# Score maxima six items ahead instead of four, with the turn one key tile earlier, in a gated cross-attention kernel

## The reference, cut to what matters

```
q = (query @ Wq).reshape(b, sq, 32, 32).transpose(0, 2, 1, 3)
k = (key @ Wk).reshape(b, sk, 8, 32).transpose(0, 2, 1, 3)
v = (value @ Wv).reshape(b, sk, 8, 32).transpose(0, 2, 1, 3)
k, v = repeat(k, 4), repeat(v, 4)
scores = einsum('bhqd,bhkd->bhqk', q, k) * 32 ** -0.5
probs = softmax(scores)
out = einsum('bhqk,bhkd->bhqd', probs, v)
```

## Time and profile before

| | |
|---|---|
| median of 3 runs | 966.67 us |
| runs | 962.91, 966.88, 966.67 us |
| profiled execution | 963.45 us, span 961.6 us |
| busy in the span | PE 875.3, DVE 667.5, POOL 527.4, ACT 421.4 us |
| mean granted TensorE clock | 0.973 |
| turns of attention (L1399) | first at 393.6, last at 788.8 us |

### The profile page before, as it was taken

The page is one execution under the profiler, slowest core; times in us unless marked ns, Lnnn a source line. Parts: engine busy times, 40 slices in busy tenths (PEclk is TensorE's granted clock), DMA queues, the critical chain, the costliest instruction groups (busy, mean ns, idle before and its releaser), DMA issues.

```text
span 961.6 us, 15794 instructions
## 1 busy us (share of the span) xinstructions
PE 875.3 (91%) x4784; PEld 353.9 (37%) x4784; DVE 667.5 (69%) x974; ACT 421.4 (44%) x730; POOL 527.4 (55%) x236
## 2 busy tenths in 40 slices
PE   3988998858889989699999999999999998999998
PEld 2656746323344434122222222222222221444443
DVE  4789867899875479677778777777778860155522
ACT  3333423433131112376776767777767777011000
POOL 4322345585330034378788888888888888321200
PEclk9999999878999999799999999999999999999999
DMA  5942222011111265234455445554444444222342
GB/s 176 354 161 88 103 88 66 1 45 44 44 55 67 85 183 164 64 86 94 103 118 118 96 97 118 118 118 107 101 96 107 103 88 88 44 45 44 55 131 76
DMA packets 68857, 94.69 MB, mean 98 GB/s; under 512 B 33360, under 2 KB 53840, under 8 KB 64720
## 3 DMA queue, kind: packets, MB, share of 16 engines
q1 hardware_dynamic: 64208, 60.58, 21.0%
q0 software_dynamic: 4608, 33.56, 17.3%
HBM read 41.55 MB, written 12.58 MB: 56 GB/s over the span
## 4 chain that ended last, share of the span: by engine, by line
PE 60%; DVE 21%; DVEq 7%; issue 7%; DMA 3%; ACT 1%; SPq 1%; POOL 0%; ACTq 0%; POOLq 0%
PE sbank L1419 10%; PE sbank L1428 10%; PE mpair L1370 9%; DVEq L778 6%; DVE mx L1062 5%; PE sbank L1215 4%; PE sbank L1216 3%; PE sbank L1217 3%; PE sbank L1505 3%; PE sbank L1509 3%; PE sbank L1507 3%; PE sbank L1520 3%; PE sbank L1522 3%; PE sbank L1438 2%; DMA regD<-mT 1%
## 5 line engine op out<-in xcount | busy, mean ns | idle before, releaser
L1062 DVE TENSOR_REDUCE mx<-mpair 128x1 f32<-128x1024 f32 (+1 forms) x256 | 301.4, 1215 | 77.3 <-PE mpair L1370 75.7
L724 ACT ACTIVATE regC<-sbank 128x512 f32<-128x512 f32 x512 | 279.7, 595 | 131.9 <-PE sbank L1419 131.3
L1419 PE MATMUL sbank<-regD 98*128 98x512 f16 x512 | 179.7, 388 | 8.6 <-DMA regD<-mT 4.4
L1370 PE MATMUL mpair<-regD 96*128 96x512 f16 x512 | 157.5, 385 | 9.9 <-issue 3.7
L483 POOL TENSOR_TENSOR wraw<-regC 128x2048 f32<-128x2048 f32 x32 | 145.2, 4539 | 22.3 <-ACT regC L724 16.4
L1428 PE MATMUL sbank<-regC,regD 128*32 128x512 f32 x1024 | 137.2, 608 | 1.0 <-ACT regC L724 1.0
L1419 PEld LDWEIGHTS sbank<-regD 98*128 98x128 f16 x512 | 46.6, 97 | 201.0 <-ACT regC L724 163.7
L483 POOL TENSOR_TENSOR regD<-regC 128x2048 f32<-128x2048 f32 x16 | 72.8, 4550 | 27.3 <-ACT regC L724 27.3
L483 POOL TENSOR_TENSOR tail<-regC 128x2048 f32<-128x2048 f32 x16 | 76.7, 4794 | 0.8 <-ACT regC L724 0.8
L1370 PEld LDWEIGHTS mpair<-regD 96*128 96x128 f16 (+1 forms) x512 | 49.0, 99 | 63.0 <-issue 11.1
L428 POOL TENSOR_SCALAR wraw<-wraw 128x1024 f32<-128x1024 f32 x16 | 17.6, 1100 | 86.9 <-ACT regR L662 79.2
(11 more groups left out here) (160 smaller groups left out, 1367.1 us busy)
## 6 DMA issues: line engine op xcount, KB each, us to landing
regD<-wraw POOLq DMA_DIRECT2D x16, 1024.0 KB, 7.0
tail<-wraw POOLq DMA_DIRECT2D x16, 1024.0 KB, 7.0
xT_lo<-in_ctx SPq DMA_DIRECT2D x16, 512.0 KB, 5.6
wraw<-in_L_ffn_W_int SPq DMA_DIRECT2D x8, 512.0 KB, 6.7
wraw<-in_L_xattn_Wq SPq DMA_DIRECT2D x8, 512.0 KB, 3.3
regD<-q_hi_scratch SPq DMA_DIRECT2D x32, 128.0 KB, 2.4
wraw<-in_L_xattn_Wo SPq DMA_DIRECT2D x8, 512.0 KB, 3.5
out<-X SPq DMA_DIRECT2D x16, 256.0 KB, 2.0
```

Source lines behind the costliest of these rows:

```text
L724: nc.scalar.activation(probs[:, kt % 4, h, :], bank[4 + h % 2], ACT.Exp, scale=SCALE).then_inc(s["exp_ok"], 1)
L1062: v.tensor_reduce(mx[m][:, bass.ds(n, 1)] if par is not None else mx[m][:, n:n + 1], slot[:, :, :], AX.XY, ALU.max).then_inc(s["mx_red"], 1)
L1370: m = pe.matmul(mpair[slot][:, half, :], qst[par][0:96, bass.ds(n * P, P)], kst[par][0:96, half * 512:(half + 1) * 512], start=True, stop= ...
L1419: pe.matmul(bank[4 + h % 2], kst[par][0:98, kt * P:(kt + 1) * P], qst[par][0:98, h * 512:(h + 1) * 512], start=True, stop=True).then_inc(s ...
```

## The change

LEAD becomes 6. In group g TensorE computes items 6 to 15 of group g + 1 in key tiles 0 to 4 and items 0 to 5 of group g + 2 in key tiles 5 to 7: item 0 beside the turn in side 1 of key tile 5, item 1 in side 0 of key tile 6, then two each in side 1 of key tiles 6 and 7. The turn and the wait for the staged operands of group g + 2 move from key tile 6 to key tile 5. The wait on `mt_cp` stands ahead of item 1 wherever it is computed. On VectorE the two parts of `invert` move: part 0 behind item 15 and ahead of `split_max`, part 1 behind item 1 of the next series.

```diff
-        LEAD = 4
+        LEAD = 6
...
                 for n in range(LEAD, ITEMS):
                     if ahead >= 1:
                         reduce_item(g + 1, nxt, n)
-                    if not first and n == ITEMS - 3:
-                        invert(g - 1, 0)
-                        invert(g - 1, 1)
+                if not first:
+                    invert(g - 1, 0)
                 if ahead >= 1:
                     split_max(g + 1, cur, g // 3 + 1)
                 for n in range(LEAD):
                     if ahead >= 2:
                         reduce_item(g + 2, far, n)
+                    if not first and n == 1:
+                        invert(g - 1, 1)
...
                 def half(kt, side):
-                    items = [todo.pop(0) for _ in range(2 * side) if todo]
+                    count = 1 if (kt, side) in ((5, 1), (6, 0)) else 2 * side
+                    items = [todo.pop(0) for _ in range(count) if todo]
                     score(g, cur, kt, 2 * side, first)
-                    if side == 1 and kt == 6 and ahead >= 1:
+                    if side == 1 and kt == 5 and ahead >= 1:
                         turn_max(g + 1, nxt)
                     if items:
                         dg, par, n = items[0]
+                        if dg == 2 and n == 1:
+                            pe.wait_ge(s["mt_cp"], g + 2)
                         pe.wait_ge(s["mx_red"], ITEMS * (g + dg) + n - 1)
                         max_half(par, n, n % 2, 0)
...
-                    if kt == 6 and ahead >= 2:
+                    if kt == 5 and ahead >= 2:
                         pe.wait_ge(stg[far], 112 * ((g + 2) // 3 + 1))
```

## The result

The changed kernel takes 967.8 us in the median of 22 runs, the kernel before 965.5 in 22: a ratio of 1.0033, with a 95% interval of 1.0019 to 1.0047. The forecast was 956. By this interval the change makes the kernel slower by 1.8 to 4.5 us. The profiled execution took 965.78 us with a span of 964.0. One of ten executions of a variant further down (the kernel before with its second transfer cut) took 1071.85 us at a mean granted clock of 0.81 and is left out of that variant's ratio.

The account below looks back on a forecast made before the run. TensorE's order and ScalarE's exponentials hold the regular tile almost equally; TensorE's waits at the turn were the loss. 6.0 + 0.3 + 3.1 + 0.8 - 1.0 = 9.2 us off gives 954.2 (profile) or 957.5 (median): 956, range 951 to 962.5.

Parts of the forecast that it names:

- (a): Sixth key tile: with two maxima items run earlier, the turn waits for no reduction; 0.36 us of waiting goes.
- (b): Seventh tile, wait for the split: 0.17 of 0.39 us stays; third score at 3.27 instead of 2.88.
- (c): VectorE's division cut in two, second half behind the second far item: new TensorE stall of 0.15 us in the eighth tile.
- Gain 0.46 a group: Steady group, (a) to (c) together: next group's first tile at 9.16 against 9.62 us; 6.0 over 13 groups.
- (d): Maxima row's transfer issued at 1.5, not 4.7: late-row waits vanish, gaining 3.1 us, and 0.8 at the last turn.
- (e): Ahead of the first group, two more maxima items delay the first score: 1.0 us lost, bounds 0.5 to 2.7.
- TensorE's clock stays at the lower level after 409: Start of attention: a sign named beforehand that would show the prediction wrong; the lower level is 1.2 GHz.
- second rival: Seventh tile and item 5: new stalls total 0.78, not 0.32 us, so (a) to (c) give nothing; 962 us, chance 0.23.
- third rival: VectorE's reciprocal shut out by GpSimd's addition: stall 2.8 us in place of 0.15 a group; 990 us, chance 0.04.

## Why the prediction was wrong

- **(a), two items earlier: right.** The turn waits for no reduction in the steady groups; the 0.36 went.
- **(b), the pair around the turn: right.** The seventh tile's third score comes at 3.17 (forecast 3.27), its second maxima item at 1.39 (forecast 1.53).
- **(c), the division cut in two: right for VectorE and TensorE, wrong in its sum.** From reciprocal to next reduction 0.96 (607.83 to 608.79; forecast 0.97), no lock, next group at 8.99 (forecast 9.16). What failed is "Gain 0.46 a group": the argument for it looked at GpSimd only for what it needs from the division (there at 4.8, needed at 6.44), and never closed the circle of its two transfers. Its sum of some 25.8 could have been read from the trace of before. The forecast period was 25.7, and TensorE reaches 25.6 once the circle is shortened. With the circle at 25.85 only the larger counts: 0.30 a group, in the better of two rhythms, and some 0.05 in the other. In periods 5 to 13 that made 1.0 us where 9 x 0.46 = 4.1 were forecast.
- **(d), the maxima row: wrong in sign.** "The transfer now travels beside a 1 MB accumulation; the earlier one did too" is the step that failed. Before, it was issued 4.8 us behind it; now it is 1.5 behind in the second and third period and 0.5 behind in the slower rhythm, and it lands with it. It goes first only in the steady groups of the first profile and in the last groups of both. Behind group 0 TensorE's matmuls waited for the row 3.5 us in all in the first profile and 9.0 in the second, against 3.0 and 1.7 in the two of the kernel before. In place of 3.1 us gained, periods 1 to 4 lose 1.7, part of it by the clock that fell in the second profile. With the transfer held back until the split, periods 2 to 4 were 2.1 shorter than before, so the earlier issue was worth something, and landing beside the 1 MB transfer took it away.
- **(e), ahead of group 0: right in size**, 1.0 forecast, 0.95 measured to the first probs times V, in two profiles each that differ by 0.9 in the kernel before. The clock's part stands behind that point: to the end of the first period it is 39.6 and 39.2 before and 40.8 twice in the changed kernel, 1.4 more, still within the bounds of 0.5 to 2.7. The lower level ended at 409.5 and 409.0 in the changed kernel, at 405.7 and 407.5 before. So the named sign "TensorE's clock stays at the lower level after 409" came in the first profile.
- **Not foreseen: the last two periods, +2.35.** 0.8 was to be gained there. The late landing (3.39 and 3.88 us of waiting, in period 14) and period 15, which took 24.7 to 25.0 before and takes the circle's 25.8 now, make the loss.

By these the sum of the two profiles each is +3.9 us. The timed runs give 2.3 by the medians and 1.8 to 4.5 by the interval; a sum of two profiles is no closer than that. The second rival, "the wait only moves", was nearest in kind, but put the new wait on VectorE; it was GpSimd's circle and the row. The wait behind GpSimd's addition that the third rival describes is real, and spared this kernel by the kind of instruction alone: at the same place the reciprocal takes 0.25 and the multiplication 2.80.

Open: why the first transfer and the row settle in one order in one execution and in the other in the next, and why the second transfer of period 14 lands late.

## What to carry to other kernels

When a change takes a wait off the engine that is busiest, add up every closed circle through a shared buffer (write, transfer, landing, next write), on the engines that look idle too: 22.2 busy of 26.1 us hid a circle of some 25.8. A small transfer that is moved earlier may be moved right behind a large one; look at what is in the queues at its new place. And a stand-in instruction in an experiment must be checked for its own duration first.

## What the runs showed of the hardware

- GpSimd's drain lasted until the accumulating transfer issued before it had landed. In the second profile of the changed kernel the multiplication came 7.2 to 9.1 us behind the issue, in thirteen groups always 0.28 behind the landing; in the run without the drain it came 6.27 behind the issue and directly behind its own predecessor.
- A transfer of 4 KB took 1.7 us to land (median) in the run in which it went ahead of one of 1 MB, and up to 7.6 right behind one in the changed kernel's second profile.
- A multiplication of 128 x 16 numbers on VectorE took 2.80 us beside GpSimd's addition, a reciprocal of the same numbers 0.254.
- A clock of 1.00 held at a period of 25.6 in which TensorE was recorded busy for 279.4 of 280 us; it was 0.54 in a stretch behind a wait of 2.01 us in the run without the reciprocal, and 0.50 in a stretch behind a wait of 1.61 us in the changed kernel's second profile.
